# Reordering the weight preparation and one step of the last stage in a four-stage transformer kernel

## What is computed

```
x = x + L0_xattn(layernorm(x), ctx)     # attention over the context, one head, fp32
x = x + L0_ffn(layernorm(x))            # three blocks of two 256x256 linears
x = x + L1_xattn(ctx, layernorm(x))     # attention with 16 heads of 16
x = x + L1_ffn(layernorm(x))            # quantised linears 256 -> 1024 -> 256, ternary weights
```

## Time and profile before

| What | Value |
|---|---|
| Median of 3 runs | 1267.38 us (1264.49 to 1268.34) |
| The profiled execution's own time | 1262.24 us |
| Its span, first to last instruction | 1260.3 us |
| TensorE busy | 1074.0 us (85%) |
| VectorE busy | 865.5 us (69%) |
| ScalarE, GpSimd busy | 529.4 us, 515.5 us |
| Mean granted TensorE clock | 0.941 of full speed |

### The profile page before, as it was taken

How to read it: one execution, slowest core, us unless ns; L and a number is a source line. 1 busy time by engine, 2 the same in 40 slices (tenths; PEclk the granted TensorE clock), 3 DMA queues, 4 the chain that set the end, 5 groups by cost and what they waited for, 6 DMA issues and landing times.

```text
span 1260.3 us, 30832 instructions
## 1 busy us (share of the span) xinstructions
PE 1074.0 (85%) x9234; PEld 772.4 (61%) x9234; DVE 865.5 (69%) x2318; ACT 529.4 (42%) x953; POOL 515.5 (41%) x875
## 2 busy tenths in 40 slices
PE   2599999999999698989886489999999999766665
PEld 2477777777777556566654246666666666434443
DVE  2846665556656467676656488888888888388886
ACT  1332222222222211111113336666666666578886
POOL 0324444444444222221210224454555554566664
PEclk7699999999999899999898869999999999779898
DMA  9423333333332000000002797777878776630000
GB/s 214 127 71 88 90 91 91 91 91 91 91 89 81 18 1 0 0 0 0 1 1 50 155 159 149 157 160 159 156 163 161 159 157 139 206 118 25 25 25 29
DMA packets 121313, 116.06 MB, mean 92 GB/s; under 512 B 45075, under 2 KB 114230, under 8 KB 121270
## 3 DMA queue, kind: packets, MB, share of 16 engines
q1 hardware_dynamic: 121270, 115.55, 39.1%
HBM read 79.15 MB, written 36.00 MB: 91 GB/s over the span
## 4 chain that ended last, share of the span: by engine, by line
PE 48%; DVE 20%; issue 11%; ACT 9%; SPq 6%; DMA 3%; POOL 2%; DVEq 2%; POOLq 0%; ACTq 0%
PE bank L1495 25%; DVE nm L1281 7%; PE bank L1653 6%; PE bank L1589 3%; ACT v_all L1006 3%; ACT v_all L999 2%; ACT v_all L993 2%; DVE hT L1200 2%; PE bank L1765 2%; PE bank L1578 2%; DVE yn L1189 2%; PE bank L1735 1%; PE bank L1751 1%; POOL rs L706 1%; PE bank L1828 1%
## 5 line engine op out<-in xcount | busy, mean ns | idle before, releaser
L1281 DVE TENSOR_REDUCE nm<-bank 112x1 f32<-112x375 f32 x512 | 247.3, 537 | 14.9 <-PE bank L1735 14.2
L954 ACT ACTIVATE pT<-bank 125x448 f32<-125x448 f32 x384 | 185.0, 543 | 54.6 <-PE bank L1751 53.8
L1735 PE MATMUL bank<-ks,qs 96*128 96x375 bf16 x512 | 166.8, 338 | 24.2 <-DMA qs<-q_parts_dram 19.4
L1751 PE MATMUL bank<-qs,ks 128*128 128x112 bf16 x1536 | 138.0, 213 | 0.6 <-DMA qs<-mrow 0.6
L1751 PEld LDWEIGHTS bank<-qs,ks 128*128 128x128 bf16 x1536 | 112.2, 99 | 21.7 <-issue 1.0
L1765 PE MATMUL bank<-pT,vaug 125*32 125x112 f32 x3072 | 100.1, 263 | 0.0
L905 ACT ACTIVATE yT<-bank,bcol,gcol 128x448 f32<-128x448 f32 x48 | 32.2, 721 | 159.9 <-PE bank L1635 159.9
L1653 PE MATMUL bank<-wffT,hT 128*112 128x256 f32 x384 | 99.1, 391 | 0.0
L1495 PE MATMUL bank<-wv1T,ctxT 128*125 128x256 f32 x384 | 88.0, 379 | 0.0
L1495 PE MATMUL bank<-ctxT,wk1T 128*128 128x375 f32 x256 | 86.0, 478 | 0.0
L1765 PEld LDWEIGHTS bank<-pT,vaug 125*32 125x32 f32 x3072 | 69.2, 109 | 24.0 <-issue 15.9
(11 more groups left out here) (204 smaller groups left out, 2288.7 us busy)
## 6 DMA issues: line engine op xcount, KB each, us to landing
k_parts_dram<-kp SPq DMA_DIRECT2D x192, 93.8 KB, 3.5
ks<-k_parts_dram SPq DMA_DIRECT2D x64, 281.2 KB, 4.2
cnat<-in_ctx_dram SPq DMA_DIRECT2D x32, 375.0 KB
ks<-k_parts_dram SPq DMA_DIRECT2D x64, 187.5 KB, 3.9
ks<-k_parts_dram SPq DMA_DIRECT2D x64, 93.8 KB, 3.4
q_parts_dram<-qp SPq DMA_DIRECT2D x48, 112.0 KB, 2.2
qs<-q_parts_dram SPq DMA_DIRECT2D x64, 84.0 KB, 4.0
x_stream<-in_x_dram SPq DMA_DIRECT2D x4, 896.0 KB, 14.9
```

Source lines behind the costliest of these rows:

```text
L954: act.activation(pT[:, u % 6, :], B3[u % 3][0:TP], ACT.Exp).then_inc(probs_made, 1)
L1281: dve.tensor_reduce(nm[:, h:h + 1], A3[h % 3][0:L], AX_X, ALU.max, negate=True).then_inc(head_max_taken, 1)
L1735: mm(A3[h % 3], qs[par][0:KS, h * L:h * L + P], ks[par][0:KS, h * T:(h + 1) * T], start=True, stop=True).then_inc(max_scores_made, 1)
L1751: last = mm(B3[c][:, j * L:(j + 1) * L], ks[par][:, h * T + c * TP:h * T + c * TP + P], qs[par][:, h * L:(h + 1) * L], start=True, stop=True)
```

## The change

It edits the preparation, the first two batches of the first attention, and the last stage.

1. SyncE loads only the first 8 batches of x early (`first_x_loaded`); the other three transfers of x (`x_loaded`) come last, behind the context of the first two batches.
2. The order in between is: lora_b, lora_a and scales in one transfer each (`ffn1_small_loaded`, three transfers), the integers in three transfers instead of six, the two last weights, the six transfers of second attention weights, then the biases and columns, which have a semaphore of their own (`ffn1_cols_loaded`). Ten small transfers and three larger ones are gone.
3. VectorE takes the statistics of 8 batches in the preparation. The other 24 are taken 12 after batch 0 and 12 after batch 1 of the first attention, behind that batch's `keep2`. GpSimd makes their factors after batch 1's work.
4. TensorE and ScalarE do lora_b, adapters and dequantised weights right behind Wv, then the sum of the absolute weights, and only then the four second attention weights and the ternary ones. VectorE adds the adapters before the ternary weights, and splits the biases last.
5. In the last stage `round_x` of a tile is done at the end of the VectorE step before (`round_x(i + 3)` in step i), and ScalarE does `xq_out` ahead of `hq_out`.
6. Three semaphores that nobody waits for become one.

The diff, cut to its core:

```diff
-        W_DEQ = 9 + NLIN // 2 + NLIN
-        W_SUMS = W_DEQ
+        W_DEQ = 5 + NLIN // 2 + NLIN
+        W_SUMS = W_DEQ + NLIN
+        XFIRST = B // 4
...
+            load_x(0)
+            sp.dma_start(rlb, L0_ffn_lora_b.rearrange("i (k p) r -> p i k r", p=P)).then_inc(ffn1_small_loaded, 16)
+            sp.dma_start(rla[0:R], L0_ffn_lora_a.rearrange("i r d -> r i d")).then_inc(ffn1_small_loaded, 16)
+            sp.dma_start(rsc, L0_ffn_scales.rearrange("i (k p) g -> p i k g", p=P)).then_inc(ffn1_small_loaded, 16)
+            for i in range(0, NLIN, 2):
+                sp.dma_start(rqi[:, i:i + 2], L0_ffn_qweights[i:i + 2].rearrange("i (k p) d -> p i k d", p=P)).then_inc(ffn1_q_loaded, 16)
+            sp.dma_start(rw1, ...)
+            sp.dma_start(rw2, ...)
...
             load_ctx(0, 0, 0)
             load_ctx(1, 1, 0)
+            for n in range(1, 4):
+                load_x(n)
...
+            x_factors(slice(0, XFIRST), XFIRST, 5)
...
+                if isinstance(b, int) and b == 1:
+                    x_factors(slice(XFIRST, B), B, 9)
...
             def step4(i, par, n):
+                if not isinstance(i, int) or i < NT - 2:
+                    xq_out(i + 2, par)
                 if not isinstance(i, int) or i >= 2:
                     hq_out(i - 2)
-                if not isinstance(i, int) or i < NT - 2:
-                    xq_out(i + 2, par)
...
+            def x_stats(first, end):
+                base = chain[0]
+                for b in range(first, end):
+                    dve.bn_stats(bst[:, b, :], xs[:, b, :]).then_inc(dve_setup_steps, 1)
+                chain[0] += end - first
+                for b in range(first, end):
+                    dve.wait_ge(dve_setup_steps, base + b - first + 1)
+                    dve.bn_aggr(mvx[:, b, :], bst[:, b, :]).then_inc(x_stats_made, 1)
+            dve.wait_ge(first_x_loaded, 16)
+            x_stats(0, XFIRST)
...
+            def step1_and_stats(b, par, n):
+                step1(b, par, n)
+                if isinstance(b, int) and b < 2:
+                    if b == 0:
+                        dve.wait_ge(x_loaded, 48)
+                    half = (B - XFIRST) // 2
+                    x_stats(XFIRST + b * half, XFIRST + (b + 1) * half)
+            over_batches(dve, step1_and_stats)
...
-                if not isinstance(i, int) or i < NT - 2:
-                    round_x(i + 2, par)
...
                 if more:
                     factor_x(i + 3, 1 - par)
                     inverse_x(i + 3, 1 - par)
+                    round_x(i + 3, 1 - par)
```

More of the change, by code:

```diff
@@ L428, in _ @@
             sp.dma_start(rwo1, L1_xattn_w_out.rearrange("(k p) d -> p k d", p=P)).then_inc(attn2_w_loaded, 16)
[L429 to L435, removed]
+            sp.dma_start(rb1[0:1], L0_ffn_biases.rearrange("(k two) d -> two k d", two=2)[0:1]).then_inc(ffn1_cols_loaded, 16)
             with nc.allow_non_contiguous_dma(reason="small columns of biases"):
                 for k in range(NBLK):
[L438 to L442, removed]
+                    sp.dma_start(b2col[:, k], L0_ffn_biases[2 * k + 1].rearrange("(c p) -> p c", p=P)).then_inc(ffn1_cols_loaded, 16)
+                    sp.dma_start(gcol[:, k], L0_ffn_ln_gamma[k].rearrange("(c p) -> p c", p=P)).then_inc(ffn1_cols_loaded, 16)
+                    sp.dma_start(bcol[:, k], L0_ffn_ln_beta[k].rearrange("(c p) -> p c", p=P)).then_inc(ffn1_cols_loaded, 16)
             def everywhere(dst, vec, n):
@@ L853, in _ @@
             leave(bqbk[:, :], jb()[:, 0:1])
-            for dst in (wvT0, wk1T, wv1T, wq1T, woT):
-                leave(dst[:, :, :], jb().rearrange("p (k d) -> p k d", k=KC))
+            leave(wvT0[:, :, :], jb().rearrange("p (k d) -> p k d", k=KC))
             for i in range(NLIN // 2):
                 leave(lbT[0:R, 2 * i:2 * i + 2], jb()[0:R, :].rearrange("p (k d) -> p k d", k=2))
+            for i in range(NLIN):
+                leave(wffT[:, i], jb().rearrange("p (k d) -> p k d", k=KC))
             act.wait_ge(ffn2_w_loaded, 32)
@@ L861, in _ @@
             act.activation(wjunk, rw2.rearrange("p k d -> p (k d)"), ACT.Abs, accum_out=wabs[:, 1:2]).then_inc(abs_w_summed, 1)
-            for i in range(NLIN):
-                leave(wffT[:, i], jb().rearrange("p (k d) -> p k d", k=KC))
             job[0] += NLIN
@@ L867, in _ @@
             act.sem_inc(weight_job_copied, NLIN)
+            for dst in (wk1T, wv1T, wq1T, woT):
+                leave(dst[:, :, :], jb().rearrange("p (k d) -> p k d", k=KC))
             for k in range(KC):
@@ L1043, in _ @@
             last.then_inc(bk_spread, 1)
[L1044 to L1053 removed]
+            def x_stats(first, end):
[8 more added lines that the diff above has]
+            x_stats(0, XFIRST)
+            dve.wait_ge(ffn1_q_loaded, 16 * (NLIN // 2))
+            dve.wait_ge(ffn1_small_loaded, 48)
             for i in range(NLIN):
@@ L1456, in _ @@
             inverse_x(2, 0)
+            round_x(2, 0)
             late = CH * (NCH - 1) - 3
@@ L1541, in _ @@
                 done(last)
-            o = jb()
-            assert job[0] == W_SUMS
-            pe.wait_ge(abs_w_summed, 2)
-            mm(o[:, 0:2], onesf, wabs, start=True, stop=True).then_inc(abs_w_total_made, 1)
-            pe.wait_ge(abs_w_mean_made, 1)
             for i in range(NLIN):
@@ L1553, in _ @@
                 done(last)
+            o = jb()
+            assert job[0] == W_SUMS
+            pe.wait_ge(abs_w_summed, 2)
+            mm(o[:, 0:2], onesf, wabs, start=True, stop=True).then_inc(abs_w_total_made, 1)
+            pe.wait_ge(abs_w_mean_made, 1)
+            pe.wait_ge(attn2_w_loaded, 96)
+            transposed(rwkv1[:, 0:KC])
+            transposed(rwkv1[:, KC:2 * KC])
+            transposed(rwq1)
+            transposed(rwo1)
             pe.wait_ge(ternary_w_made, 1)
```

69 lines of the change are left out of this document (29 added, 40 removed).

## The result

The changed kernel takes 1260.03 us (median of 12 runs, 1252.89 to 1263.05), the kernel before 1267.26 us beside it (12 runs). The ratio is 0.994 (95% interval 0.9921 to 0.996): 7.2 us less by the medians. Faster was right, and 1260.03 lies in the range, but of the 12.5 us that I forecast only some 7 came.

A forecast was written before the change was run, and what follows sets the result against it. Transfers bound the preparation, TensorE the first attention, and a loop with no engine full the last stage. -20.2 + 8.5 + 4.7 - 5.5 = -12.5 us gave a median of 1254.9 us against 1267.38, range 1246 to 1265.

The forecast's parts named there:

- The start, -20.2: Preparation: the first attention starts at 48 us instead of 68.2, 20.2 us gained, bounds 46.1 and 52 us.
- columns and broadcasts 2 us, to 30: Preparation's transfers: columns and broadcasts take 2 us after the second attention weights at 28, ending at 30 us.
- The rival of late quarters: Preparation: x lands at 55 us, bias rows wait behind it, start at 56, total 1262.9 us; chance 0.14.
- my main case: Whole kernel: start at 48 us, 12.5 us gained, median 1254.9 us; chance 0.58, own range 1249 to 1261.
- Statistics, 8.5 lost: First attention: statistics blocks of 4.8 us stall TensorE 4.0 us behind batch 0 and 4.55 behind batch 1.
- Clock, 4.7 lost: First attention: TensorE at half speed after pauses, 3.0 us lost at its beginning and 1.7 for the two stalls.
- The last stage, -5.5: Last stage: earlier `round_x` brings tiles from 5.47 to 5.25 us, 5.1 us, plus 0.4 for an early `activate`.
- the two-tile loop: Last stage: the next limiting loop, `activate` through `round_h`, turns, `xq_out` and 3.51 us, 10.3 to 10.7 us per two tiles.
- The power of 24 batches: First attention, batch 2: GpSimd's factors cost nothing; as a rival, they hold VectorE, +3.5 us, 1258.4; chance 0.07.
- the rule that the prediction cites: First attention: GpSimd and a VectorE operation with two SBUF inputs exclude each other; total would be 3.5 us worse.
- The unmoved last stage: Last stage: tiles don't get faster because the new loop is as long as the old; total 1260.4 us; chance 0.12.
- the collision: Last stage: `round_h` and `round_x` meet GpSimd operations, tiles 5.95 us, 13.4 us lost, total 1273.8; chance 0.09.

The follow-up runs named there:

- columns_last: Changed kernel with the nine column transfers issued after the bias rows and the biases' source loaded with the adapters: 1255.89 us, 0.9922 of the kernel before.
- bias_rows_other_queue: Changed kernel with the three bias rows issued by ScalarE on its own queue: 1254.88 us, 0.9921 of the kernel before.
- The mended version: Changed kernel with statistics row by row, bias rows and broadcasts earlier, columns behind `stage_end`, old `hq_out`/`xq_out` order: 1231.72 us, 0.9732 of the kernel before.
- the repeat: Changed kernel measured once more, unchanged, on the chip of the last group of runs: 1260.03 us, 0.9949 of the kernel before.
- tensor_engine_kept_busy: Changed kernel with 15 unused matmuls added in TensorE's pause ahead of the first attention: 1255.70 us, 0.9928 of the kernel before.
- stats_row_by_row: Changed kernel with the last 24 batches' statistics and factors made one batch at a time, and `nmr1` subtracted without sign change: 1254.56 us, 0.9908 of the kernel before.
- the last stage alone: Kernel before with only the edits of the last stage: 1260.42 us, 0.997 of the kernel before.
- the order alone: Kernel before with only `xq_out` put ahead of `hq_out` in the last stage: 1292.30 us, 1.0211 of the kernel before.

## Why the prediction was right or wrong

**The start, -20.2: the step that failed.** It was 13.3 us, at 54.9 instead of 48, beyond the bound of 52 that I had named as a sign of being wrong. The work on VectorE, TensorE and ScalarE was right within 3 us (split of the biases at 41.3 against 41.7). The failed step is "columns and broadcasts 2 us, to 30". They took 10 us, from 28 to 38, and held x behind them on the queue. I had written that such columns "hardly use the engines", which is true (share 0.32 to 0.53), and drew the wrong end from it: they still hold up what is queued behind them. The prediction itself put "some 5 us" on the same columns in the kernel before, and then 2 us on them and the broadcasts together. Two stretches of the kernel before, in which SyncE had these columns under way, show what they do:

```profile
36.00:38.00 2.00, 0.00 (x0) 0.00 (x0) 1.64 (x26) 0.00 (x0) 0.27 (x1) 0.50 0.28 6
38.00:40.00 2.00, 0.00 (x0) 0.00 (x0) 0.00 (x0) 0.00 (x0) 1.92 (x2) 0.50 0.24 2
```

A second part failed too: I had the three rows issued in 1.86 us and landed 2.6 us later; behind and beside x the issues took 5.1 us and the landing 6.6 us. `columns_last` won 4.7 us of the start back and `bias_rows_other_queue` 6.6. The mended version won 11.8, but it also splits the biases early, issues their rows ahead of the contexts and x, and moves the broadcasts, so its gain is not the columns' alone.

**The rival of late quarters** had the place right (bias rows behind x, start at 56) and gave 1262.9. It named x's own rate as the cause, and that was wrong: x started about 8 us late and its last quarter landed at about 54 (issued at 40.14, 13 to 14 us to land), some 7 after my 47. The start lay nearer to this rival than to my main case.

**Statistics, 8.5 lost.** Stalls of 3.41 and 4.35 us, 7.8: right. In the repeat they were 3.41 and 4.36.

**Clock, 4.7 lost.** Mis-sized: 4.6 us in batch 0 (I had 3.0, for a pause of 6 us that became 15.9) and 1.8 us behind each of the two stalls (15.98 - 10.76 - 3.41, and 16.93 - 10.77 - 4.35) where I had one drop for both. That is 8.2 us. In the repeat it was 9.1: batches of 13.6, 17.3 and 17.7 us. `tensor_engine_kept_busy` shows the first, the 11.4 us of `stats_row_by_row` stalls and clock of the blocks together (7.8 + 3.6).

**The sum for the preparation** so becomes -13.3 + 7.8 + 8.2 = +2.7 in the profiles, against -7.0. The medians say +1.0 alone and, as the difference between the kernel after (-7.2 and -6.5) and the last stage alone (-5.0), about -2. The intervals of these runs are some 2 us wide on either side; which of them is nearer stays open. Either way the 7.0 us did not come.

**The last stage, -5.5.** -5.0 alone, and 5.14 us a tile against 5.25: the size was right, the reason half wrong. I counted `xq_out` ahead of `hq_out` as part of the gain; it costs 4 to 5 of the 10 us that the rounding brings. The terms that I listed for the two-tile loop add up to 10.3 to 10.6 us, not 10.7, so the upper bound should have been 5.28 a tile. The steady tiles gained 0.30 us each and not 0.22, and the first interval between two `result`s gave some of it back: 6.85 us instead of 5.40, with a granted clock of 0.50 from 1110 to 1120 us where before had 0.72.

**The other rivals.** The power of 24 batches (4.20 us) ran at 99.58, later than I thought, and `kr` beside it took 0.94 us, as in batches 0 and 1; there was no third stall. No operation of VectorE with two SBUF operands stood beside it, so the rule that the prediction cites was not tried by the kernel after. The unmoved last stage and the collision are refuted by the tiles of 5.14 us: `round_h` met something only twice in the stage's first 30 us (1.60 and 1.00 us) and takes 0.76 after it. The price of a worse loop, though, is real, by another mechanism than the rival's: 25.8 us with the order alone.

That the kernel came out faster was in part luck. The sum of 12.5 us had room for an error of 7 us in the start and of 3.5 to 4.4 in the clock. In the median 5.0 of the 7 us are the last stage, and nearly all of the preparation's gain is gone.

## What to carry to other kernels

Price small scattered transfers by the time for which they hold their queue (here 10 us with the broadcasts), not by their bytes, and put those that nobody needs soon behind the point at which all engines meet, not only behind the other transfers. When an edit makes TensorE ready earlier than its data, count the pause and the half clock behind it; here filling the pause was worth 4.6 us of the first batch, and closing it 3.9 beside 7.7 of start. Before two instructions of an in-order engine change places, ask which of them is ready first: the one that waits takes the other's cover with it.

## What the runs showed of the hardware

In the kernel after, the copy of two numbers (L1117) took 1.03 us from 86.35, and GpSimd's product with it ended at 87.36; the same copy beside the power took 0.16 us. Timeline of both:

```profile
85.85 1.51 POOL L674 TENSOR_TENSOR kp<-kr,kp 128x750 bf16<-128x750 f32 x1
...
86.35 1.03 DVE L1117 COPY mvx<-mvb 112x2 f32<-112x2 f32 x1
```

```profile
99.58 4.20 POOL L641 TENSOR_TENSOR rs<-nmr,minus_half 112x24 f32<-112x24 f32 x1
...
103.29 0.16 DVE L1117 COPY mvx<-mvb 112x2 f32 x1
```

The Trainium skill, "SBUF — State Buffer", section "SBUF: two separate sides", lets a GpSimd operation and a VectorE operation in a two-port mode, or with two SBUF inputs, exclude each other for a whole instruction. If the copy runs in such a mode, which no view here shows, the first pair agrees and the second does not. The second pair is weak, since spans on GpSimd are rough and the copy begins 0.49 us before the power ends; the prediction's row, VectorE products of 0.38 us each in the last 1.9 us of a power of 5.47 us, says the same more firmly.

Fifteen matmuls without use, put into the pause, took 4.6 us off the first batch and 4.6 us off the span of the profiled execution.
